# Recommendation tower: which pair of tiles skips the late lookups, and the order of the last pair's layers

## The reference

```
e = stack([tbl_f[ids[:, f]] for f in range(26)], axis=1)
x = concatenate([bottom[:, None], e], axis=1)        # 2048 x 27 x 128
z = einsum('bfd,bgd->bfg', x, x)[:, upper triangle]  # 2048 x 351
h = relu(concatenate([z, bottom], 1) @ W_top1 + b_top1)   # 479 -> 512
h = relu(h @ W_top2 + b_top2)                             # 512 -> 256
y = h @ W_top3                                            # 256 -> 1
```

## Time and profile before

| what | value |
|---|---|
| device time, median of 3 runs | 382.97 us (382.36 to 384.99) |
| the profiled execution's own time | 382.43 us |
| its span, first to last instruction | 380.7 us |
| mean granted TensorE clock | 0.991 |
| PE (matmuls) | busy 348.3 us, 91% |
| DVE (VectorE) | busy 261.8 us, 69% |
| POOL (GpSimd) | busy 263.8 us, 69% |
| ACT (ScalarE) | busy 117.8 us, 31% |
| HBM read | 31.50 MB, 83 GB/s |

### The profile page before, as it was taken

How to read it: one execution, slowest core, us unless ns; L and a number is a source line. 1 busy time by engine, 2 the same in 40 slices (tenths; PEclk the granted TensorE clock), 3 DMA queues, 4 the chain that set the end, 5 groups by cost and what they waited for, 6 DMA issues and landing times.

```text
span 380.7 us, 14045 instructions
## 1 busy us (share of the span) xinstructions
PE 348.3 (91%) x6112; PEld 311.4 (82%) x6112; DVE 261.8 (69%) x781; ACT 117.8 (31%) x218; POOL 263.8 (69%) x281
## 2 busy tenths in 40 slices
PE   0879869999998999989998999989999899999997
PEld 0767759898887999978887898978998799887886
DVE  4999998985757957566537866677767586723232
ACT  3453641333223322313232341313323133132311
POOL 5777777777777777777777777777777777775000
PEclk9999998999999999999999999999999899999999
DMA  7755574332242312212331322413123212121000
GB/s 229 198 148 205 173 236 163 94 85 55 54 97 58 92 51 57 79 50 59 98 92 50 94 54 54 106 51 91 50 58 99 57 50 57 52 57 46 4 2 1
DMA packets 16684, 32.42 MB, mean 85 GB/s; under 512 B 5488, under 2 KB 8176, under 8 KB 16496
## 3 DMA queue, kind: packets, MB, share of 16 engines
q0 software_dynamic: 8704, 17.84, 18.4%
q1 hardware_dynamic: 7920, 13.69, 11.6%
HBM read 31.50 MB, written 0.01 MB: 83 GB/s over the span
## 4 chain that ended last, share of the span: by engine, by line
PE 80%; DVE 15%; DMA 3%; issue 1%; ACT 1%; SPq 0%; ACTq 0%; DVEq 0%
PE hot_ps L366 36%; DVE onehot L496 11%; PE gram_ps L346 11%; PE h_ps L407 10%; PE h_ps L419 8%; PE xt_ps L329 7%; PE h_ps L404 5%; DVE tab L545 3%; DMA stage_sb<-in_hot_dram 3%; PE zt_ps L385 2%; DVE h L535 1%; PE hot_ps L407 0%; ACT tab L633 0%; DMA ids_wide<-in_hot_ids_dram 0%; DVE Z L504 0%
## 5 line engine op out<-in xcount | busy, mean ns | idle before, releaser
L318 POOL DMA_INDIRECT X<-in_table_dram,rows_sb x272 | 262.4, 965 | 84.3 <-issue 81.1
L496 DVE TENSOR_SCALAR onehot<-ids_wide,row_value 128x256 fp32r<-128x256 int16 x640 | 199.5, 379 | 81.4 <-PE hot_ps L366 78.5
L366 PE MATMUL hot_ps<-onehot,tab 128*128 128x256 f32 x1280 | 191.9, 298 | 13.7 <-DVE onehot L496 13.5
L366 PEld LDWEIGHTS hot_ps<-onehot,tab 128*128 128x128 f32 x1280 | 166.7, 194 | 20.4 <-issue 13.3
L475 ACT COPY XT<-xt_ps 128x512 f32<-128x512 f32 x64 | 38.9, 608 | 165.2 <-PE xt_ps L329 165.2
L346 PEld LDWEIGHTS gram_ps<-XT 128*27 128x27 f32 x4096 | 40.6, 105 | 23.1 <-issue 14.8
L346 PE MATMUL gram_ps<-XT 128*27 128x26 f32 x4096 | 53.5, 190 | 4.4 <-DVE Z L504 3.2
L604 ACT COPY XT<-hot_ps 128x256 f32<-128x256 f32 x72 | 49.4, 686 | 25.1 <-PE hot_ps L366 24.7
L407 PE MATMUL h_ps<-stage_sb,w_sb 128*128 128x256 f32 (+3 forms) x198 | 45.1, 363 | 0.0
L329 PE MATMUL xt_ps<-ident,X 128*128 128x128 f32 x272 | 40.8, 272 | 2.1 <-ACT XT L471 1.9
L419 PE MATMUL h_ps<-w_sb,stage_sb 128*128 128x256 f32 x128 | 32.9, 402 | 9.3 <-DVE h L535 9.3
(11 more groups left out here) (32 smaller groups left out, 59.6 us busy)
## 6 DMA issues: line engine op xcount, KB each, us to landing
ids_wide<-in_hot_ids_dram SPq DMA_DIRECT2D x14, 320.0 KB
X<-in_table_dram,rows_sb POOLq DMA_INDIRECT x272
stage_sb<-in_hot_dram SPq DMA_DIRECT2D x15, 256.0 KB, 4.2
stage_sb<-in_hot_dram SPq DMA_DIRECT2D x10, 192.0 KB, 3.1
bottomT<-in_bottom_t_dram SPq DMA_DIRECT2D x8, 128.0 KB, 4.1
w_sb<-in_w_dram SPq DMA_DIRECT2D x1, 1024.0 KB
w_sb<-in_w_dram SPq DMA_DIRECT2D x1, 512.0 KB, 9.2
vec_sb<-in_vecs_dram SPq DMA_DIRECT2D x1, 256.0 KB, 9.3
```

The source lines that it names most:

```text
L318: pool.indirect_dma_start(X[:, n % RING, k, :], None, table, bass.IndirectOffsetOnAxis(idx[:, column:column + 1], 0)).then_inc(gathered[n ...
L366: mm = pe.matmul(hot_ps[i % 2][:, 0:WIDE], tab[u][:, part, D * c:D * (c + 1)], onehot[p % ONEHOTS][:, c - PIECE[u][h], :], start=(c == 0 a ...
L496: compared = dve.tensor_scalar(onehot[p % ONEHOTS][:, c - PIECE[u][h], :], ids_wide[:, u, :], row_value[:, c:c + 1], None, ALU.is_equal)
```

## The change

HOTS gives the 6 lookups to pairs 0 and 1 and 10 to all others (before: pairs 0 and 4). Totals of compares, lookup matmuls, units and gathers are the same. The late tables' 12 pieces are split two in each of steps 0 to 5. On VectorE layer3 of an odd tile's last step goes behind the first of the freed one-hots, not behind all. From step 56 on TensorE has an order of its own (`last_step`): in each step the Gram block stands ahead of the next unit's transposes; layer 1 of the job (12, 13) ends in step 60, layer2(12) is in step 61, all of layer 1 of tile 14 and layer2(13) in step 62, layer2(14) in step 63 ahead of the last Gram block. VectorE does layer3(12) and layer3(13) in steps 62 and 63 and layer3(14) ahead of z_transpose(15); ScalarE's ReLUs follow.

```diff
@@ -34,11 +34,14 @@
 BOTTOMS = 6
 PIECE_MAX = 4
 RUNS = 2
+SPLIT_STEPS = 6
 GROUPS_PER_BANK = 16
 CHUNKS = [min(P, PAIRS - P * c) for c in range(-(-PAIRS // P))]
 
 GROUPS = TILES // 2
-HOTS = [HOT_BASE, HOT, HOT, HOT, HOT_BASE, HOT, HOT, HOT]
+LAST = 2 * BLOCKS * (GROUPS - 1)
+HOTS = [HOT_BASE, HOT_BASE, HOT, HOT, HOT, HOT, HOT, HOT]
+LATE = HOTS.index(HOT)
 FIRST = [sum(HOTS[:n]) for n in range(GROUPS + 1)]
 LOOKUPS = [(n, u) for n in range(GROUPS) for u in range(HOTS[n])]
 UNITS = []
@@ -104,6 +107,8 @@
     PIECE_OF = [(u, h) for u in range(HOT) for h in range(len(PIECE[u]) - 1)]
     ASKED = [(i, u, h) for i, (n, u) in enumerate(LOOKUPS) for h in range(len(PIECE[u]) - 1)]
     ASKED_AT = {(i, h): p for p, (i, u, h) in enumerate(ASKED)}
+    LATE_PIECES = list(range(FIRST_PIECE[HOT_BASE], FIRST_PIECE[HOT]))
+    PER_STEP = -(-len(LATE_PIECES) // SPLIT_STEPS)
     PRODUCTS = [[PARTS * sum(HC[:u]) for u in range(h + 1)] for h in HOTS]
     SLICES = RUNS * BLOCKS * 2
 
@@ -359,7 +364,7 @@
                     h = sum(1 for begin in PIECE[u][1:] if begin <= c)
                     p = ASKED_AT[i, h]
                     if part == 0 and c == PIECE[u][h]:
-                        if n < 2:
+                        if n <= LATE:
                             pe.wait_ge(part0, FIRST_PIECE[u] + h + 1)
                             pe.wait_ge(part1, FIRST_PIECE[u] + h + 1)
                         pe.wait_ge(onehot_ready, p + 1)
@@ -425,9 +430,6 @@
                 g = t // 2 - 1
                 if j == 1 and t > 0:
                     z_transposes(t - 1)
-                if t == TILES - 1 and j >= 2:
-                    layer1(len(JOBS) - 2, 2 * (j - 2))
-                    layer1(len(JOBS) - 2, 2 * (j - 2) + 1)
                 if g >= 0:
                     if t % 2 == 0 and j >= 2:
                         layer1(g, j - 2)
@@ -448,16 +450,53 @@
                     gram(b, run)
                 mlp(b // BLOCKS, b % BLOCKS)
 
+            def last_step(b):
+                j = b % BLOCKS
+                if b < TILES * BLOCKS - BLOCKS:
+                    gram_block(b)
+                    next_units(b)
+                    mlp(b // BLOCKS, j)
+                if b == TILES * BLOCKS - BLOCKS:
+                    gram_block(b)
+                    next_units(b)
+                    layer1(len(JOBS) - 3, 2)
+                    layer1(len(JOBS) - 3, 3)
+                if b == TILES * BLOCKS - BLOCKS + 1:
+                    gram_block(b)
+                    next_units(b)
+                    z_transposes(TILES - 2)
+                    layer2(TILES - 4)
+                if b == TILES * BLOCKS - BLOCKS + 2:
+                    gram_block(b)
+                    layer1(len(JOBS) - 2, 0)
+                    layer1(len(JOBS) - 2, 1)
+                    next_units(b)
+                    layer1(len(JOBS) - 2, 2)
+                    layer1(len(JOBS) - 2, 3)
+                    layer2(TILES - 3)
+                if b == TILES * BLOCKS - 1:
+                    layer2(TILES - 2)
+                    gram_block(b)
+
+            def gram_block(b):
+                for run in range(RUNS):
+                    gram(b, run)
+
+            def next_units(b):
+                for n in UNITS_OF.get(b + 1, []):
+                    transposes(n)
+
             pe.wait_ge(ident_ready, 1)
             pe.wait_ge(pads_zero, 2)
             for u in range(HOT_BASE):
                 lookups(0, PRODUCTS[0][u], PRODUCTS[0][u + 1])
                 if u >= 3 and u - 3 in UNITS_OF[0]:
                     transposes(u - 3)
-            for b in range(TILES * BLOCKS):
+            for b in range(LAST):
                 step(b)
+            for b in range(LAST, TILES * BLOCKS):
+                last_step(b)
             z_transposes(TILES - 1)
-            layer2(TILES - 2)
             for c in range(C1):
                 layer1(len(JOBS) - 1, c)
             layer2(TILES - 1)
@@ -522,6 +561,8 @@
 
                 g, at = JOB_OF[t]
                 dve.wait_ge(zt_full, t + 1)
+                if t == 0:
+                    dve.wait_ge(part1, FIRST_PIECE[HOT])
                 wait(dve, h1_full, C1 * (g - 1))
                 dve.tensor_copy(ZT[g % 2][:, :, at, :],
                                 zt_ps[:, 0:len(CHUNKS) * P].rearrange("p (c s) -> p c s", s=P)).then_inc(zt_moved, 1)
@@ -551,16 +592,19 @@
                     z_transpose(t - 1)
                 if j == 2 and t > 0:
                     move_zt(t - 1)
-                for p in pieces_ended(b):
+                freed = pieces_ended(b)
+                for p in freed[:1]:
+                    one_hot(p + ONEHOTS)
+                if t >= 3 and t % 2 == 1 and j == 3 and t < TILES - 1:
+                    layer3(t - 3)
+                if t == TILES - 1 and j >= 2:
+                    layer3(t - 5 + j)
+                for p in freed[1:]:
                     one_hot(p + ONEHOTS)
                 if j == 0 and t > 0:
                     fold(t - 1)
-                if b < SOMETIMES:
-                    u = HOT_BASE + b
-                    for q in range(FIRST_PIECE[u], FIRST_PIECE[u + 1]):
-                        split_second(q)
-                if t >= 3 and t % 2 == 1 and j == 3:
-                    layer3(t - 3)
+                for q in LATE_PIECES[PER_STEP * b:PER_STEP * (b + 1)]:
+                    split_second(q)
                 if t >= 4 and t % 2 == 0 and j == 0:
                     layer3(t - 3)
 
@@ -582,11 +626,10 @@
                 one_hot(p)
             for b in range(TILES * BLOCKS):
                 step(b)
+            layer3(TILES - 2)
             z_transpose(TILES - 1)
             fold(TILES - 1)
-            layer3(TILES - 3)
             move_zt(TILES - 1)
-            layer3(TILES - 2)
             layer3(TILES - 1)
 
         @block.scalar
@@ -638,25 +681,26 @@
                 if g >= 0 and t % 2 == 1 and j == 0:
                     relu(g, 0)
                     relu(g, 1)
-                if g >= 0 and t % 2 == 1 and j == 2:
+                if g >= 0 and t % 2 == 1 and j == (1 if t == TILES - 1 else 2):
                     relu(g, 2)
                     relu(g, 3)
 
             def step(b):
                 t, j = b // BLOCKS, b % BLOCKS
                 relus(t, j)
+                if b == TILES * BLOCKS - 2:
+                    relu(len(JOBS) - 2, 0)
+                    relu(len(JOBS) - 2, 1)
                 moves(b + 1)
+                if b == TILES * BLOCKS - 2:
+                    relu(len(JOBS) - 2, 2)
+                    relu(len(JOBS) - 2, 3)
                 for i in ended(b):
                     place_hot(i)
                 if j == 2:
                     place_bottom(t + 1)
-                if b < SOMETIMES:
-                    u = HOT_BASE + b
-                    for q in range(FIRST_PIECE[u], FIRST_PIECE[u + 1]):
-                        split_first(q)
-                if t == TILES - 1 and j >= 2:
-                    relu(len(JOBS) - 2, 2 * (j - 2))
-                    relu(len(JOBS) - 2, 2 * (j - 2) + 1)
+                for q in LATE_PIECES[PER_STEP * b:PER_STEP * (b + 1)]:
+                    split_first(q)
 
             for u in range(HOT_BASE):
                 for q in range(FIRST_PIECE[u], FIRST_PIECE[u + 1]):
```

## The result

The changed kernel took 390.97 us by the median of four runs (387.56 to 392.79), the kernel before 382.67 beside it: ratio 1.0195, 95% interval 1.011 to 1.0281. It is slower by about 2%. The profiled execution was the shortest of the four, 387.56 us with a span of 385.7.

A forecast was written before the change was run, and what follows sets the result against it. PE's own work was taken to set the middle's pace, with POOL's gathers (272 x 1.27 us) a second clock. 3.8 + 8.3 - 9.1 + 0.3 + 0 + 3.6 + 0.6 = +7.5 on 382.4 gave 389.9 us, range 385.0 to 394.0.

The forecast's parts named there:

- Gathers, +3.8: Up to step 11's last transposes: PE needs 17 units, not 15, and cannot be there before 93.4 us; +3.8 us.
- Pair 3, +8.3: Lookups moved to pair 3 add 8.85 us there; one unit of transposes leaves pair 4, 0.60; sum +8.3 us.
- layer3, -9.1: End of odd tiles: with layer3 earlier on DVE, PE's five waits at L419 go; -9.1 us.
- margin of half a microsecond for the Z transpose: After odd tiles: Z ready near 119.7 us, next gram asks at 120.2; cost taken as 0, otherwise 5 x 0.5.
- Late tables, +0.3: Blocks 0 to 5: six instead of four may slow gathers lying on a DVE split; 0 to 0.6, taken +0.3 us.
- Last pair, +3.6: Behind gram(63) nothing covers DVE's chain; layer2(14) to last layer1 takes 6.15 us instead of 1.83; +3.6 us.
- Clock, +0.6: PE half-speed stretches: one goes with its L419 wait, new waits may bring others; -1.7 to +1.7, taken +0.6 us.
- The first: Rival: the end and the clock cost nothing; +1.6, 384.0 us; 17%.
- the second: Rival: PE, not the gathers, sets pairs 0 and 1; 17th unit at 78.1 us, total 374.6 us; 5%.
- the third: Rival: the moved layer3 fails, layer2 or gram still waits for DVE; all 9.1 back, 399.0 us; 5%.
- The fourth: Rival: the clock follows every long wait; three more half-speed stretches, 5 us, 395 us; 10%.

The follow-up runs named there:

- e1: The kernel before with the change of HOTS alone (6 lookups for pairs 0 and 1): 398.46 us against 382.92, ratio 1.0428.
- e5: The changed kernel with the last pair's old order put back on PE, DVE and ACT: 384.52 us, ratio to the kernel before 1.0045.
- e6: The changed kernel with layer3 of odd tiles' last step put back behind all one-hots, last pair's new order kept: 402.86 us against 382.92, ratio 1.054.
- e9: The changed kernel with only the last Gram block and its chain moved ahead of the second half of tile 14's layer 1: 384.63 us, ratio 1.008.
- e7: The changed kernel with one more wait on POOL ahead of its first gather, so gathers start late: 398.46 us, kernel before beside it 382.2.
- e4: The changed kernel with the HOTS of before put back, all else of the change kept: 375.41 us against 382.42, ratio 0.9812.
- e2: The kernel before with layer3 moved ahead of all but the first freed one-hots, nothing else: 373.38 us against 382.92, ratio 0.9771.
- e8: The kernel before with one more wait on POOL ahead of its first gather, so gathers start late: 389.27 us against 382.42, ratio 1.0154.

## Why the prediction was right, point by point

The forecast was 389.9 us, the median is 391.0. By its own steps:

**Gathers, +3.8.** The profile shows 93.15 - 89.62 = +3.5. Step 12 follows 6.07 us later without a wait, as forecast. In the traces of e1, e5, e6 and e9, which have the new HOTS too, the 17th unit stands at 93.33 to 93.86, and in e7 it moves with POOL's start. I had forecast some 15 us of idle before the transposes; it was 12.2, since PE also worked at half speed there.

**Pair 3, +8.3.** Pairs 2 and 3 are alike now, 44.65 us, where I wrote 44.6. e1 and e4 give HOTS as a whole 15.5 and 15.6, against 12.1 from the two terms. In e1 the rest is two stretches at half speed; for e4 that is not shown. e5 against e2 gives 11.1.

**layer3, -9.1.** The waits are gone, e2 gives -9.5 alone, e6 +11.9 when it is undone. In the changed kernel nothing takes their place; in e2 the gathers do in part. The margin of half a microsecond for the Z transpose is in these rows of the changed kernel, at step 15's end:

```profile
117.78 0.40 DVE L576 TENSOR_TENSOR h<-h_ps,vec_sb 128x256 f32<-128x256 f32 x1
...
122.31 1.03 DVE L543 STREAM_TRANSPOSE Z<-gram_ps 128x832 f32<-128x832 f32 x1
...
123.79 0.42 PE L351 MATMUL gram_ps<-XT 128*27 128x26 f32 x32
```

DVE ends at 123.34, the Gram begins at 123.79.

**Late tables, +0.3.** Not so. POOL's 68th gather starts at 90.52 us in the change and at 90.84 before, 0.3 earlier instead of later, and over all traces the two splits cannot be told apart (see e4). The term should have been nothing.

**Last pair, +3.6.** From layer2(14) on it is 6.02 us for my 6.15, and 3.9 for the pair as a whole. By e5 and e9 the median gains 6.4 when the Gram block goes back, so the term was right for the wait, and the medians hold some 2.5 more that no trace of the change or of e5 shows. A stretch at half speed behind the chain, as in e6 and e7, would be 1.7 of it.

**Clock, +0.6.** The step that was mis-sized, in both directions. In the profiled execution there was no stretch where it could cost, -1.7, and 3.5 + 8.3 - 9.1 + 3.9 - 1.7 = 4.9 is its span's +5.0. By the medians the change costs 8.3; less 3.5 + 8.3 - 9.1 + 3.9 = 6.6 the clock has +1.7, nearly three times my value. That the untraced executions spend it behind the 17th unit and behind the chain is argued, not seen in them: of the six traces with the new HOTS three have a stretch right behind the 17th unit (e1, e6, e9), and of the four with the uncovered chain two have one behind it (e6, e7). Apart from the clock my terms make 6.9 and the rows 6.6; that the total came within 1.1 us of the median rests on a clock term that was picked between its bounds, and is luck to that extent. The Trainium skill's rule ("TensorE: Matmul & The Clock Gate", What's actually happening), that the slow clock is the default and activity releases it, bore out more than I gave it: these traces agree at 95.0 us in e1 and 385.0 in e7. They do not bear out the strict form, a stretch behind every long wait: four of the five waits at L419 in the earlier trace rows brought none, and neither did the uncovered chain in the change's own trace and in e4's.

**The rivals.** The first (nothing lost at the end) is refuted by the 6.02 us, the second by the 17th unit at 93.15 us instead of 78.1, the third by the waits at L419, which are gone. The fourth (the clock follows every long wait) is true in part, as just said.

## What to carry to other kernels

An engine that is busy 68% can still be the bound of a stage: look at the gaps between its instructions, and if they are all alike and wait for nothing, its issue rate is a clock. Before moving work out of a stage, lay the arrivals that the stage needs against its own pace; what is freed below that pace turns into waiting, and the work comes back in full where it is put. And where the last piece of a chain is reordered, count what still stands behind it to cover the chain.

## What the runs showed of the hardware

Waits of 1.7 to 1.9 us on PE have a second price, in some executions and not in others. The kernel before, with five of them, ran from 379.69 to 386.22 us on one chip, and its time goes with the mean granted clock: 379.69 to 380.06 us at 0.995, 381.67 to 382.92 at 0.991, 383.87 to 386.22 at 0.982. e2, without them, ran from 373.13 to 373.92 at 0.995 to 1.000. In e1 stretches of 3.4 us at 1.2 GHz follow such waits (217.8, 265.6), in e8 one at 125.0. In e2 and e4 none stands between 75 and 340 us. A half-speed stretch has a price only where PE sets the pace: 17 us of them before 88.8 us left the change's 17th unit where the gathers had it.

And one chip of those used ran all five kernels 38 to 42% slower (the kernel before 533 us for 383), at a mean granted clock of 0.88 to 0.91 in the profiled executions of e4, e7, e8 and e9 and with gaps on PE that no wait explains.
